# The fourth norm inside the delta stage, and a second FFN that loads its own late tiles

## The reference, cut to what matters

```python
def _layernorm(x, axis=-1, eps=1e-05):
    m = jnp.mean(x, axis=axis, keepdims=True)
    v = jnp.var(x, axis=axis, keepdims=True)
    return (x - m) / jnp.sqrt(v + eps)
...
x = x + _L0_attn_a_ref(_layernorm(x), Wq, Wk, Wv, Wo)      # x1
x = x + _L0_ffn_ref(_layernorm(x), ...)                     # x2, first FFN
x = x + _L0_attn_b_ref(_layernorm(x), ...)                  # x3, delta stage
x = x + _L0_ffn_ref(_layernorm(x), ...)                     # fourth norm, second FFN
```

## Time and profile before

| | us |
|---|---|
| median of 3 runs | 3374.71 (3371.95 to 3380.33) |
| the profiled execution | 3378.45 |
| its span, first to last instruction | 3376.6 |
| PE busy | 3209.5 (95%) |
| DVE busy | 2158.8 (64%) |
| ACT busy | 1519.3 (45%) |
| mean granted PE clock | 0.975 of full |

### The profile page before, as it was taken

The page is one execution under the profiler, slowest core; times in us unless marked ns, Lnnn a source line. Parts: engine busy times, 40 slices in busy tenths (PEclk is TensorE's granted clock), DMA queues, the critical chain, the costliest instruction groups (busy, mean ns, idle before and its releaser), DMA issues. The chain is left out here.

```text
span 3376.6 us, 76185 instructions
## 1 busy us (share of the span) xinstructions
PE 3209.5 (95%) x32272; PEld 1567.8 (46%) x32272; DVE 2158.8 (64%) x3596; ACT 1519.3 (45%) x3484; POOL 126.4 (4%) x458
## 2 busy tenths in 40 slices
PE   8999999996889999999999999999999869999999
PEld 4444444443444444545444454554445434444443
DVE  2454425426789888888878888898898535441541
ACT  2221102104566766676676577567667532110110
POOL 0000000000000000000000000000000000000000
PEclk9999999997999999999999999999999769999999
DMA  3022322113111111021111111111211022232121
GB/s 121 0 87 62 87 81 57 56 57 103 39 31 43 36 62 43 27 83 40 44 48 49 61 33 58 40 41 39 71 42 40 5 93 71 64 87 81 57 55 69
DMA packets 97936, 191.09 MB, mean 57 GB/s; under 512 B 10312, under 2 KB 35656, under 8 KB 95296
## 3 DMA queue, kind: packets, MB, share of 16 engines
q1 hardware_dynamic: 97600, 186.22, 18.0%
HBM read 171.25 MB, written 14.94 MB: 55 GB/s over the span
## 5 line engine op out<-in xcount | busy, mean ns | idle before, releaser
L1748 PE MATMUL psum<-dl_xt,dl_wqkv 128*128 128x512 f32 x1536 | 762.6, 620 | 9.7 <-DVE dl_qkv L1380 9.7
L1380 DVE SCALAR_TENSOR_TENSOR dl_qkv<-psum,dl_par,dl_qkv 128x511 f32<-128x511 f32 (+2 forms) x576 | 428.7, 744 | 36.8 <-ACT dl_tails L1212 27.8
L520 PE MATMUL psum<-xnt_sb,wmats 128*128 128x512 f32 x896 | 408.9, 593 | 1.1 <-DVE f_partial L788 1.1
L1748 PEld LDWEIGHTS psum<-dl_xt,dl_wqkv 128*128 128x128 f32 x1536 | 262.7, 190 | 265.2 <-issue 229.1
L520 PE MATMUL psum<-f_token_sums,wmats 128*128 128x512 f32 x672 | 306.8, 592 | 0.0
L788 DVE TENSOR_TENSOR f_partial<-f_partial,psum 128x512 f32<-128x512 f32 x112 | 76.9, 687 | 311.4 <-PE psum L520 310.0
L520 PEld LDWEIGHTS psum<-xnt_sb,wmats 128*128 128x128 f32 x896 | 169.1, 190 | 214.1 <-issue 207.9
L1755 PE MATMUL psum<-dl_wo,dl_sg 128*128 128x512 f32 x512 | 256.4, 620 | 0.4 <-DVE dl_sg L1585 0.4
L671 ACT ACTIVATE f_partial<-psum 128x512 f32<-128x512 f32 x32 | 19.1, 597 | 510.5 <-PE psum L520 510.5
L1208 ACT ACTIVATE dl_qkv<-psum,dl_par 128x512 f32<-128x512 f32 x192 | 148.9, 776 | 179.5 <-PE psum L1748 177.9
L576 PE MATMUL psum<-f_wdown,f_hidden_b 128*128 128x512 f32 x512 | 221.7, 593 | 3.4 <-DVE x_sb L811 3.4
(11 more groups left out here) (237 smaller groups left out, 4796.3 us busy)
## 6 DMA issues: line engine op xcount, KB each, us to landing
dl_wqkv<-in_dw_qkv SPq DMA_DIRECT2D x192, 256.0 KB, 2.7
f_wdown<-in_wdowns SPq DMA_DIRECT2D x64, 512.0 KB, 3.3
wmats<-in_wmats SPq DMA_DIRECT2D x56, 512.0 KB, 3.4
dl_wo<-in_dwo SPq DMA_DIRECT2D x16, 1024.0 KB, 5.3
f_weights_b<-f_weights_by_expert SPq DMA_DIRECT2D x24, 512.0 KB, 8.9
x_sb<-in_x SPq DMA_DIRECT2D x4, 1024.0 KB, 9.2
x_after_experts<-x_sb SPq DMA_DIRECT2D x16, 256.0 KB, 2.4
dl_wfb<-in_dwfb SPq DMA_DIRECT2D x16, 256.0 KB, 3.0
```

The lines of the kernel that those rows point to most:

```text
L520: ins = pe.matmul(ps[:, bank, :], wm[:, m % WRING, block, k, :], moving[:, k, :], start=(fresh and k == 0), stop=(last_of and k == 1), ski ...
L1380: tap_ = lambda dl: dve.scalar_tensor_tensor(y_[:, dl:TT], ps[:, bank, 0:TT - dl], par[:, h, 4 * a + 3 - dl:4 * a + 4 - dl], y_[:, dl:TT], ...
L1748: last = pe.matmul(ps[:, bank, :], wq[:, n % RING, m, :], xt[:, u // HG % 2, m, :], start=(m == 0), stop=(m == KC - 1))
```

## The change

1. The stage `n4_` is gone. Its work moves into the delta stage, behind each tile's last unit: after each of the four `add_rows` of such a unit DVE takes `bn_stats` and `bn_aggr`; ACT takes `Ln` and `Exp` in slot 10; DVE computes the shift and normalizes row group 0 at the end of slot 11, and groups 1, 2, 3 at the ends of slots 12, 13, 14; PE transposes them as four new small jobs `normed`; ACT copies each into `xs4`; SP stores each to `xn_transposed` in DRAM.
2. A store of `xs4` must have landed before the next copy into it. For the last tile, results go to free parts of `qkv` instead.
3. The load of the next tile's rows moves from slot 9 to slot 1 of the next unit.
4. In the last unit SP loads the second FFN's router, its first matrix (into the free ring of projection weights) and the normalized tiles 0 and 1 (into `dl_xt`, which stays allocated).
5. The second FFN loads tiles 2 and 3 and matrices 1 and 2 first thing in its own block, and the residual rows (one DMA of 4 MB) behind its router weights' spread. Its logits move from ahead of matrix 0 to behind that matrix's third product; DVE's order in matrix 0 follows.
6. To make room: `zd` has one buffer, `bnt` lies in `small`, and `junk`, the unused output of ACT's 256 squares, lies in psum bank 3.

```diff
@@ short_jobs
     jobs += table.get((sl, at), [])
+    normed = {(12, "end"): 0, (13, "end"): 1, (15, "long"): 2, (15, "end"): 3}.get((sl, at))
+    if normed is not None and p >= 0 and p % HG == HG - 1:
+        jobs = jobs + [("normed", p, normed, every)]
@@ delta_stage, SP
+                def store_normed(u, n):
+                    i = u // HG
+                    wait_read(sp, "normed", u, n)
+                    if i == 2:
+                        sp.wait_ge(s["xt_in"], 16 * 2)
+                    sp.dma_start(xnt_dram[i][:, :, P * n:P * n + P], staged(u, n)).then_inc(s["xn4_stored"], 16)
...
+                        if sl >= 13 and p >= 0 and p % HG == HG - 1:
+                            store_normed(p, sl - 13)
...
+                        if sl == 2 and k == UNITS - 1:
+                            wait_full(sp, "proj", k, 11)
+                            sp.wait_ge(s["xn4_stored"], 16 * 8)
+                            experts_early(sp)
+                            for n in range(2):
+                                sp.dma_start(xt[:, n], xnt_dram[n]).then_inc(s["xt_in"], 16)
@@ delta_stage, ACT
+                    elif kind == "normed":
+                        wait_full(act, *job)
+                        if u < UNITS - 1 and (u >= HG or n > 0):
+                            act.wait_ge(s["xn4_stored"], 16 * (4 * (u // HG) + n))
+                        act.activation(staged(u, n), ps[:, bank, :].rearrange("p (k t) -> p k t", k=KC), ACT.Copy).then_inc(read[bank], 1)
...
+                        if sl == 10 and post and p % HG == HG - 1:
+                            act.wait_ge(s["var4_ready"], 4 * (p // HG) + 4)
+                            if not prep:
+                                act.preload_act_table_set("natural_log_exp_and_others")
+                            o.done(act.activation(nrs[:, :], nmv[:, :, 1], ACT.Ln, bias=eps5))
+                            o.wait()
+                            act.activation(nrs[:, :], nrs[:, :], ACT.Exp, scale=-0.5).then_inc(s["std4_ready"], 1)
@@ delta_stage, DVE, add_rows
                     dve.tensor_tensor(xr[:, n, :], ps[:, bank, :], xr[:, n, :], ALU.add).then_inc(read[bank], 1)
+                    if u % HG == HG - 1:
+                        wait_read(dve, "rows", u, n)
+                        step(dve.bn_stats(nst[:, n, :], xr[:, n, :]))
+                        dve.bn_aggr(nmv[:, n, :], nst[:, n, :]).then_inc(s["var4_ready"], 1)
...
+                        if post and p % HG == HG - 1 and sl == 11:
+                            norm_shift(p)
+                        if post and p % HG == HG - 1 and 11 <= sl < 15:
+                            normalize(p, sl - 11)
@@ ffn_stage, PE
                     multiply(m, BC, 4, ts[:, 0], True, False)
-                    if m == 0:
+                    if m == 0 and rows_in is None:
                         turn_logits()
+                    elif m == 0:
+                        logits()
...
                     multiply(m, BB, 2, t3, False, False)
+                    if m == 0 and rows_in is not None:
+                        turn_logits()
@@ program
-            norm_stage(nc, "n4_", x_sb, xnt, ps, cst, source=x3, ahead=ahead)
-            ffn_stage(nc, "f2_", x_sb, xnt, ps, cst, d, out, loaded)
+            def ahead(sp):
+                for n in range(2):
+                    sp.dma_start(late[:, n], xnt_dram[2 + n]).then_inc(late_in, 16)
+                weights_ahead(sp)
+            ffn_stage(nc, "f2_", x_sb, [xt[:, 0], xt[:, 1], late[:, 0], late[:, 1]], ps, cst, d, out, loaded, ahead=ahead,
+                      x_in=(x3_in, late_in), rows_in=x3)
```

More of the change, by code:

```diff
@@ L443, in ffn_stage @@
         BA, BB, BC = 0, 1, 2
-        tokens = lambda p, side: slice((2 * p + side) * FT, (2 * p + side) * FT + FT)
+        weight = lambda m, b: wm_first[:, b] if wm_first is not None and m == 0 and b < 4 else wm[:, m % WRING, b]
+        half = lambda p, side, n: tiles[2 * p + side][:, 2 * n:2 * n + 2, :]
         group_mats = lambda p, g: (MATS * p + g,) if g < SG else (MATS * p + 2 * g - SG, MATS * p + 2 * g - SG + 1)
@@ L481, in _ @@
                     sp.dma_start(dst[:], dram[name]).then_inc(w_in, 16)
+                if x_in[0] is not None:
+                    ahead(sp)
                 for i in range(4):
@@ L485, in _ @@
                     load_down(q)
-                if ahead is not None:
+                if ahead is not None and x_in[0] is None:
                     ahead(sp)
@@ L585, in bias, with logits @@
                         pe.matmul(ps[:, 4 + i, :], wt[rows, e, :], bd[rows, :], start=False, stop=True).then_inc(acc_ps, 1)
+                def logits():
+                    if rows_in is not None:
+                        pe.wait_ge(x_in[1], 32)
+                    for k in range(KC):
+                        for s in range(FN):
+                            last = pe.matmul(ps[32 * s:32 * s + NE, 4, :], wr[:, k, :], tiles[s][:, k, :],
+                                             start=(k == 0), stop=(k == KC - 1), skip_group_check=True)
+                    last.then_inc(logits_ps, 1)
                 def turn_logits():
@@ L608, in _ @@
                 pe.wait_ge(wr_in, 32)
[L609 to L612, removed]
-                last.then_inc(logits_ps, 1)
+                if rows_in is None:
+                    logits()
                 products(0)
@@ L1056, in delta_stage @@
         mid = slice(P, 2 * P)
+        junk = ps[:, 3, mid]
         place = place_jobs()
@@ L1828, in short_job @@
                                              start=(m == 0), stop=(m == KC - 1))
+                    elif kind == "normed":
+                        pe.wait_ge(s["xn4_ready"], 4 * (u // HG) + n + 1)
+                        for m in range(KC):
+                            last = pe.transpose(ps[:, bank, P * m:P * m + P], normed(u, n)[:, P * m:P * m + P], ident)
                     elif kind == "turn":
```

131 lines of the change are left out of this document (87 added, 44 removed).

## The result

| | median us | runs (lowest to highest) | ratio to the kernel before |
|---|---|---|---|
| before, in the same comparison | 3376.44 | 6 (3371.95 to 3380.33) | |
| changed | 3390.49 | 6 (3388.23 to 3393.64) | 1.0039 [1.0029, 1.005] |

The account below looks back on a forecast made before the run. PE was taken to bound the delta stage but not the seam. Three tiles at 10.5 us (+31.5) minus 21.5 for the seam gave +10 on 3374.71, 3384.7, shaded to 3384; range 3362 to 3397.

Parts of the forecast that it names:

- Seam: Delta stage to second FFN: its block starts 25.3 us earlier, matrix 0 loses 3.8; net gain 21.5 us.
- rival of the weak seam: Delta stage to second FFN: stores land late and late tiles come 3 us later; gain 17, 3389 us; chance 0.13.
- PE's transposes: Delta stage, PE full: four transposed row groups cost 1.8 us per tile; covered entirely, 0.
- first rival: Delta stage: `corner`'s wait takes nothing from the end; 3365 us, or 3360 if transposes also fit into gaps; chance 0.12.
- DVE ahead of the residual of slot 12: Slot 9's statistics, the shift and first normalize delay slot 12's residual; 1.8 us per tile, bounds 0 and 2.3.
- Slot 13's bank wait: Slot 13: the second `normed` waits for the bank of ACT's `krow` copy; 0.5 us per tile.
- `corner`'s stop: Slot 15: `corner` waits for ACT's third `normed` copy behind table load and Exp; 3.7 us per tile, bounds 3.1 and 4.5.
- Clock: Delta stage: low clock after PE's stops; 1.7 us for the 3.7 us stop, 1.0 for the 3.3 us one, per tile.
- Other edits at nothing: Stores, load order, single `zd` buffer and `junk` in psum: taken as 0, no more than 3 us either way.
- stops hidden: Delta stage: PE works ahead of the chain, the clock stays up; a tile costs 4.1 us, total 3365; chance 0.12.
- no tile cost: Delta stage: the tiles cost nothing, only the gain between the stages remains; 3353 us; chance 0.05.
- The clock stays low: Delta stage: one 10.1 us low-clock stretch per tile, 13 to 14 us per tile; 3394 us; chance 0.20.

Follow-up runs that it names:

- Experiment 5: On top of experiment 2: shift and first normalize moved behind slot 12's residual and add_state, SP issues the late tiles first; 3368.87 us, ratio 0.9978.
- experiment 7: On top of experiment 2: ACT's four copies of the first three tiles cut to 16 of 512 columns; 3373.96 us, one run.
- experiment 1: Kernel before, with only `corner` in steps 4, 8 and 12 made to wait for a later ACT copy; 3395.37 us, ratio 1.0059.
- experiment 2: Changed kernel with ACT's copy of the third `normed` taken ahead of slot 15's table load and Exp; 3372.8 us, ratio 0.999.
- experiment 8: Changed kernel with ACT's copy of the third `normed` between slot 15's table load and the Exp; 3382.25 us, ratio 1.0017.
- experiment 4: Changed kernel without the norm of the first three tiles, the seam and all other edits kept; 3355.5 us, ratio 0.9936.
- experiment 6: On top of experiment 2: three of four transposes left out of each `normed` of the first three tiles; 3372.73 us, one run.
- experiment 3: Changed kernel with the third `normed` in slot 14 instead of slot 15; 3381.55 us, ratio 1.0013.

## Why the prediction was right, step by step

The forecast was 6.5 under the measured median, inside its range, and the sign was the likeliest one. Both halves of the sum hold: the stop behind the Exp is there, uncovered, and the seam gives what it was to give. Of the 6.5, 1.7 come from the base (the kernel before measured 3376.4 in six runs, and the forecast was added to the 3374.7 of three), 0.7 from rounding down and 4.1 from the sum. That the sum comes so near is in part luck: three terms of the tiles are off, and the one that was too high cancels half of the two that were too low.

- *Seam*: advance 25.3 predicted, from the block's start at 12.6 after the start of the last `add_rows`; measured 12.75, so an advance of 25.2. Landing of a store 2.7 predicted, 2.6 measured. Matrix 0 was to lose 3.8; from the block's start to the last `join` it is 22.9 instead of 18.7, so 4.2. Logits at 9.7 predicted, 9.5 measured. Net 21.5 against 21.0. (Four products at the prediction's own 1.78 are 7.1 and not 6.9, which moves the 21.5 by 0.2.) The rival of the weak seam was wrong, although its 3389 is nearer to the measured time than my sum: the time alone could not have told them apart.
- *PE's transposes*: 1.8 per tile. Three of four give back 1.3, so about 1.75 in all. Right, and the covering that the first rival needed is not there.
- *DVE ahead of the residual of slot 12*: 1.8 predicted; 1.5, 0.5 and 1.2 measured, 1.1 on average, so the term was too high by 0.7. PE's wait was to be 3.3 and is 2.60, 0.93 and 2.00. Experiment 5 shows that 0.7 of the 1.5 and of the 1.2 is the shift and the first normalize; that the rest is the statistics of slot 9 is argued, not shown. The statistics of slots 6, 7 and 8 are covered, as said: the slots up to 10 don't grow.
- *Slot 13's bank wait*: 0.5 predicted for slot 13. Slot 13 itself has the transposes' 0.4 and no more. What the traces show beyond the transposes (0.44 each) and `corner`'s wait is 0.3 in slot 14, 0.3 in slot 15 and 0.3 in the slot behind. The delay was put in the wrong place, and the sum of such small delays, 0.9, was put too low by 0.4. It is not ACT's copies (experiment 7); what it is, no run shows.
- *`corner`'s stop*: 3.7 predicted, 3.64 measured, three times, with the releaser named. Experiments 1, 2 and 8 show that this wait and the clock that comes with it make the slot's growth: moved or put in alone, they move it. Nothing covers it.
- *Clock*: the step that was mis-sized. "Per tile I take 1.7 for the 3.7 us stop and 1.0 for the 3.3 us one." The sum of 2.7 rested on a stretch of 3.4 us behind a stop. Behind `corner` the stretch is 6.8 us, and it costs 7.0 - 0.7 - 3.64 = 2.7 in step 12 of the changed kernel, 2.6 on average over its three steps, and 2.8 in experiment 1. Behind slot 12's wait a stretch of 3.4 came in two steps of three, 1.6 each, 1.1 on average. Together 3.7 per tile, so the term was too low by 1.0. The earlier trace rows had no low stretch, one of 3.4 and one of 10.1, so a size for a stop of 3.7 could not be read from them; the bounds (0 to 10) held it and the value was too low.
- *Sum*: 10.5 per tile predicted, 11.0 measured (33.1 in three), the clock +1.0, the small delays +0.4, DVE -0.7 and the rest about -0.1. Net +10 predicted, +12 from tiles and seam, +14 by the medians. Of the last 2, 0.9 lies in the last step, for which I had no term; the other 1 is within what the executions vary by.
- *The shading* from 3384.7 to 3384 was for stalls that hide one another. No such hiding shows. In experiment 1 each stop costs its full length and more.
- *Other edits at nothing*: right, by experiment 4, to 0.1 per slot. The squares into psum take 281 ns instead of 310, 256 times (before, then changed; the number behind the comma is the mean in ns):

```profile
L1190 ACT ACTIVATE dl_junk<-dl_val 128x128 f32<-128x128 f32 x256 | 79.2, 310 | 23.7 <-ACT dl_val L1186 0.4
...
L1243 ACT ACTIVATE psum<-dl_val 128x128 f32<-128x128 f32 x256 | 72.0, 281 | 23.7 <-ACT dl_val L1239 0.4
```

By the Trainium skill (ScalarE: Activation LUTs, section Step-by-step: what each stage is for) ACT writes psum with less latency; the rows agree, by 29 ns. No slot became shorter for it (experiment 4).

- *The rivals*: "stops hidden" was excluded by experiment 1, "no tile cost" by the traces. "The clock stays low" (3394) had the wrong length (6.8, not 10.1), but it erred the right way, and the measured 3390.5 lies between it and my sum. The rule of the Trainium skill (Trainium Kernel Development and Optimization, section Performance Expectations), by which PE at 46% of weight loads would have had room for the transposes, does not hold in these slots: experiment 6 shows that they cost what they take, 0.3 to 0.4 for three.

## What to carry to other kernels

A small job that is added to an engine written in program order has to be followed into two places: which buffer the job takes away from the next user, and what stands ahead of the instruction that frees it. Here a copy of 0.6 us behind a table load and an Exp held PE for 3.64 in three places and cost 17.5 us, more than the kernel's whole loss of 14; taken ahead of them it holds PE for 0.42. When PE is busy nearly all the time, as here, each stop of it should be priced at its own length and at the low clock that may come with it. A single span can hide a gain of 4 us behind dips that fall elsewhere (experiment 6); the slots, taken one by one, show it.

## What the runs showed of the hardware that I had not expected

- In the delta stage, behind a stop of 3.64 to 3.73 the granted clock was 0.50 or 0.51 for 6.8 us in six cases of six (changed kernel and experiment 1). Behind one of 2.00 it was low for 3.4 in three of three (experiment 3). Behind one of 1.84 it was low for 3.4 in two of three (experiment 8). Behind the wait of 2.60 for slot 12's residual it was low for 3.4 in six of seven cases, over all the traces, and full in one (step 4 of experiment 2), with the same instructions as in step 4 of the changed kernel. Behind the waits of 1.81 to 2.08 at that place it was low in two (2.00 and 2.08) and full in four (1.81 twice, 1.90 and 1.95). So a stop of about 2 us has a price that varies from run to run: itself, or itself and 1.6.
- In experiment 6 two such dips made slot 13 of steps 4 and 12 longer by 1.6 and 1.3 than it was in step 8. That took 2.9 of the 3.9 us that the transposes gave back.
- The store of 256 KB in pieces of 512 bytes landed 2.6 us after its issue, and one of 1 MB in 4.3: a quarter of the bytes took 0.6 of the time.
